# First chunk of x in two half loads, VectorE normalising the first three chunks, three constant products ahead on TensorE

## The reference

```python
xn = (x - mean(x)) / sqrt(var(x) + 1e-5)              # per row
# recurrent part, 256 inner columns
hidden, gate = split(xn @ W_hg)
h = scan over the 256 positions of each sequence:
        h[t] = sigmoid(-gate[t]) * h[t-1] + sigmoid(gate[t]) * (relu(hidden[t]) + 0.5)
s = h @ W_out
# mixture of experts, 16 experts of width 64, the two best per row, and a shared one of width 128
shared = (silu(xn @ Sg) * (xn @ Su)) @ Sd
p = softmax(xn @ Wr);  the two largest p and their experts
routed = sum over these two: p * (silu(xn @ Wg[e]) * (xn @ Wu[e])) @ Wd[e]
out = x + s * silu(routed + shared)
```

## Time and profile before

| | |
|---|---|
| median of 3 runs | 329.79 us (329.2 to 330.83) |
| profiled execution | 327.45 us |
| its span on the core | 325.7 us |
| PE busy | 291.7 us, 90% of the span |
| DVE busy | 252.0 us, 77% |
| ACT busy | 241.4 us, 74% |
| POOL busy | 201.2 us, 62% |
| chain that ended last | PE 78%, ACT 5%, issue 5%, POOL 4%, DVE 3%, DMA 1% |

### The profile page before, as it was taken

How to read it: one execution, slowest core, us unless ns; L and a number is a source line. 1 busy time by engine, 2 the same in 40 slices (tenths; PEclk the granted TensorE clock), 3 DMA queues, 4 the chain that set the end, 5 groups by cost and what they waited for, 6 DMA issues and landing times.

```text
span 325.7 us, 5997 instructions
## 1 busy us (share of the span) xinstructions
PE 291.7 (90%) x1523; PEld 198.5 (61%) x1523; DVE 252.0 (77%) x634; ACT 241.4 (74%) x517; POOL 201.2 (62%) x242
## 2 busy tenths in 40 slices
PE   0699999999989999996968999999999999999920
PEld 0357767766656666663645676777777777777620
DVE  7399999999999799999451778787878787878830
ACT  1789999999975777985664777777787878787520
POOL 3997446530137776878667777665656566656670
PEclk9999999999998999998999999999999999999985
DMA  8999999690006885333795435755656454541000
GB/s 233 303 372 393 440 445 399 228 432 3 0 28 204 279 256 215 124 127 147 247 405 195 168 107 194 208 176 149 180 149 181 150 181 129 168 127 51 19 0 0
DMA packets 28256, 63.62 MB, mean 195 GB/s; under 512 B 3717, under 2 KB 22672, under 8 KB 27456
## 3 DMA queue, kind: packets, MB, share of 16 engines
q1 hardware_dynamic: 21184, 45.58, 41.3%
q0 software_dynamic: 6752, 17.06, 14.2%
q10 hardware_dynamic: 288, 0.60, 0.6%
HBM read 29.32 MB, written 35.14 MB: 198 GB/s over the span
## 4 chain that ended last, share of the span: by engine, by line
PE 78%; ACT 5%; issue 5%; POOL 4%; DVE 3%; DMA 1%; POOLq 0%; ACTq 0%; DVEq 0%
PE p_u L998 21%; PE p_u L926 20%; PE p_s L1023 10%; PE p_s L937 8%; PE p_sh L1010 5%; PE p_lg L907 4%; PE p_sh L946 4%; PE p_xt L974 3%; POOL out L354 2%; PE p_xt L894 2%; DMA arena<-in_x 1%; POOL arena L310 1%; ACT arena L457 1%; ACT rec L427 1%; ACT rec L420 1%
## 5 line engine op out<-in xcount | busy, mean ns | idle before, releaser
L354 POOL DMA_INDIRECT out<-arena x83 | 82.1, 989 | 46.4 <-DVE arena L825 30.0
L926 PE MATMUL p_u<-xT,w_front 128*128 128x512 f32 x192 | 93.9, 622 | 3.2 <-DVE prod L569 2.5
L348 POOL DMA_INDIRECT slots<-arena,pos x64 | 71.4, 1116 | 28.7 <-issue 16.1
L998 PE MATMUL p_u<-arena 128*128 x166 | 78.3, 593 | 0.0
L926 PEld LDWEIGHTS p_u<-xT,w_front 128*128 128x128 f32 x192 | 34.9, 198 | 35.4 <-issue 33.9
L1023 PEld LDWEIGHTS p_s<-arena,rec 128*128 128x128 f32 x332 | 43.4, 191 | 21.2 <-issue 21.2
L799 DVE TENSOR_TENSOR rec<-p_u,rec 128x512 f32<-128x512 f32 (+1 forms) x42 | 28.8, 685 | 29.3 <-ACT rec L473 29.3
L480 ACT ACTIVATE rec<-p_sh 128x512 f32<-128x512 f32 (+1 forms) x42 | 24.9, 592 | 30.8 <-PE p_sh L1010 30.8
L1023 PE MATMUL p_s<-arena,rec 128*128 x332 | 44.1, 276 | 1.3 <-ACT rec L480 1.3
L998 PEld LDWEIGHTS p_u<-arena 128*128 128x128 f32 x166 | 28.3, 190 | 19.6 <-issue 19.6
L561 DVE TENSOR_TENSOR_SCAN rec<-rec 128x512 f32<-128x512 f32 x32 | 39.3, 1229 | 1.1
(11 more groups left out here) (130 smaller groups left out, 440.5 us busy)
## 6 DMA issues: line engine op xcount, KB each, us to landing
slots<-arena SPq DMA_DIRECT2D x4, 4116.0 KB, 27.0
arena<-slots SPq DMA_DIRECT2D x41, 392.0 KB, 3.3
arena<-in_W_lines SPq DMA_DIRECT2D x2, 2304.0 KB, 11.3
arena<-in_x SPq DMA_DIRECT2D x16, 256.0 KB, 5.3
arena<-in_W_lines SPq DMA_DIRECT2D x4, 768.0 KB, 4.5
out<-arena POOLq DMA_INDIRECT x83, 2.7
slots<-arena,pos POOLq DMA_INDIRECT x64
w_front<-in_W_front ACTq DMA_DIRECT2D x1, 392.0 KB, 3.6
```

The lines of the kernel that those rows point to most:

```text
L348: pool.indirect_dma_start(slots, index, xrow[:, t], None).then_inc(s_disp[t % WINDOW], 16)
L354: pool.indirect_dma_start(out, index, xg[:, n % RX, h, X], None, bounds_check=T - 1, oob_is_err=False)\
L926: nc.tensor.matmul(p_u[:, n % 4], w_front[:, UPS[q]:UPS[q] + P], xT[:, c % XB], start=True, stop=True)\
L998: last = nc.tensor.matmul(p_u[:, n % 2 * 2 + h], xsT[:, n % 2, h * P:(h + 1) * P], w_lines[:, bass.DynSlice(line_at[2 * n + h], 4 * P)], s ...
```

## The change

1. **Chunk 0** is loaded in two halves, one by SyncE and one by ScalarE, which issues it ahead of `w_front`. The wait of `ln_stats(0)` is for both.
2. **The first three chunks** (`HEAD`) are normalised by VectorE (`normalise_first`), with NBIAS made there too. GpSimd makes only RSTD for them (`rstd_first`, two instructions for four). ScalarE normalises from chunk 3 on.
3. **TensorE** first runs three products of 128x512 of a constant (`rec_v[:, 0]`, set to 1.0 by VectorE's first instruction, `s_warm`) into `p_u`, which later work overwrites.
4. **`STATS`** is later: chunk 4 between the two scans of iteration 0, chunks 2i+3 and 2i+4 in iteration i from 1 to 4, then 13 in iteration 5, 14 in 6 and 15 in 7.
5. **GpSimd** does the small constants and a part of the blank region (4 row groups) before the first `rstd`, and VectorE zeroes 6 groups in place of 10. GpSimd's larger zeroing of 11 groups now stands behind the `rstd_of` of chunk 3 and ahead of that of chunk 4.

```diff
-        BLANK_BY_DVE = SLOTS // 8
+        BLANK_BY_DVE = 6
+        BLANK_EARLY = 4
-        STATS = {i: [2 * i + 5, 2 * i + 6] for i in range(-1, 5)} | {5: [15]}
+        STATS = {i: [2 * i + 3, 2 * i + 4] for i in range(1, 5)} | {5: [13], 6: [14], 7: [15]}
...
-            for c in range(NCH):
+            sp.dma_start(xrow[:, 0:TT // 2, X], x_tiles[0][:, 0:TT // 2]).then_inc(s_xin[0], 16)
+            for c in range(1, NCH):
                 load_x(c)
...
+            def rstd_first(c):
+                pool.wait_ge(s_mv, c + 1)
+                if c >= 1:
+                    pool.wait_ge(s_rstd, c)
+                nc.gpsimd.tensor_tensor(var_eps[:, :], meanvar[:, c, :, 1], eps[:, :], ALU.add).then_inc(s_ve, 1)
+                pool.wait_ge(s_ve, c + 1)
+                nc.gpsimd.tensor_tensor(xrow[:, c * TT:(c + 1) * TT, RSTD], var_eps[:, :], minus_half[:, :], ALU.pow)\
+                  .then_inc(s_rstd, 1)
...
-            pool.wait_ge(s_const, 3)
-            rstd_of(0)
...
-            rstd_of(1)
+            nc.gpsimd.memset(rec_a.rearrange("p j (q n) -> p (j q) n", q=2)[:, :, 0:1], 0.0).then_inc(s_const, 1)
+            nc.gpsimd.memset(blank[:, BLANK_BY_DVE:BLANK_BY_DVE + BLANK_EARLY, 0:TOKEN], 0.0).then_inc(s_blank, 1)
+            pool.wait_ge(s_const, 3)
+            rstd_first(0)
...
-            rstd_of(2)
+            rstd_first(1)
+            rstd_first(2)
...
-            nc.gpsimd.memset(blank[:, BLANK_BY_DVE:, 0:TOKEN], 0.0).then_inc(s_blank, 1)
+            rstd_of(HEAD)
+            nc.gpsimd.memset(blank[:, BLANK_BY_DVE + BLANK_EARLY:, 0:TOKEN], 0.0).then_inc(s_blank, 1)
...
+            act.dma_start(xrow[:, TT // 2:TT, X], x_tiles[0][:, TT // 2:]).then_inc(s_xin[0], 16)
...
-            normalise(0)
             copy_xT(0)
-            for c in read(0):
-                normalise(c)
...
+            def normalise_first(c):
+                k, rows = c % 4, xrow[:, c * TT:(c + 1) * TT]
+                dve.wait_ge(s_rstd, c + 1)
+                nc.vector.scalar_tensor_tensor(out=rows[:, :, NBIAS], in0=meanvar[:, k, :, 0], scalar=-1.0,
+                                               in1=rows[:, :, RSTD], op0=ALU.mult, op1=ALU.mult).then_inc(s_nb, 1)
+                dve.wait_ge(s_nb, c + 1)
+                if c >= XN:
+                    dve.wait_ge(s_xt, c - XN + 1)
+                for t in range(TT):
+                    row = xrow[:, c * TT + t]
+                    last = nc.vector.tensor_scalar(xn[:, c % XN, t], row[:, X], row[:, RSTD:RSTD + 1],
+                                                   row[:, NBIAS:NBIAS + 1], ALU.mult, ALU.add)
+                last.then_inc(s_norm, 1)
...
+            nc.vector.memset(rec_v[:, 0], 1.0).then_inc(s_warm, 1)
             nc.vector.memset(blank[:, 0:BLANK_BY_DVE, 0:TOKEN], 0.0).then_inc(s_blank, 1)
-            for c in [0] + read(0) + STATS[-1]:
-                ln_stats(c)
+            ln_stats(0)
+            normalise_first(0)
+            ln_stats(1)
+            ln_stats(2)
+            normalise_first(1)
+            ln_stats(3)
+            normalise_first(2)
...
                 rec_scan(i, 0)
+                if i == 0:
+                    ln_stats(HEAD + 1)
...
+            pe.wait_ge(s_warm, 1)
+            for n in range(3):
+                nc.tensor.matmul(p_u[:, n], rec_v[:, 0, 0:P], rec_v[:, 0], start=True, stop=True)
             pe.wait_ge(s_const, 5)
             transpose_x(0)
```

More of the change, by code:

```diff
@@ L20 @@
 FIRST = 10
+HEAD = 3
 XN = 2
@@ L203, in recurrent_moe_block @@
         s_blank, s_init = sem("blank_rows_ready"), sem("slots_blanked")
+        s_warm = sem("warm_operand_ready")
         s_xin = [sem(f"x_landed{k}") for k in range(NCH)]
@@ L266, in load_slots @@
                 sp.dma_start(xg[:, n % RX, 0:m], rows.rearrange("(h p) w -> p h w", p=P)).then_inc(s_xg[n % RX], 16)
-            for c in range(NCH):
+            sp.dma_start(xrow[:, 0:TT // 2, X], x_tiles[0][:, 0:TT // 2]).then_inc(s_xin[0], 16)
+            for c in range(1, NCH):
                 load_x(c)
-            sp.wait_ge(s_blank, 3)
+            sp.wait_ge(s_blank, 4)
             for q in range(4):
@@ L303, in rstd_of @@
                 pool.wait_ge(s_mv, c + 1)
-                if c >= 1:
-                    pool.wait_ge(s_rstd, c)
-                    pool.wait_ge(s_nb, c)
+                pool.wait_ge(s_rstd, c)
+                pool.wait_ge(s_nb, c)
                 nc.gpsimd.tensor_tensor(var_eps[:, :], meanvar[:, k, :, 1], eps[:, :], ALU.add).then_inc(s_ve, 1)
                 nc.gpsimd.tensor_tensor(minus_mean[:, :], meanvar[:, k, :, 0], minus_one[:, :], ALU.mult).then_inc(s_ve, 1)
-                pool.wait_ge(s_ve, 2 * (c + 1))
+                pool.wait_ge(s_ve, HEAD + 2 * (c - HEAD + 1))
                 nc.gpsimd.tensor_tensor(xrow[:, c * TT:(c + 1) * TT, RSTD], var_eps[:, :], minus_half[:, :], ALU.pow)\
@@ L334, in _ @@
             nc.gpsimd.memset(carry[:, :, 0:1], 0.0).then_inc(s_const, 1)
-            nc.gpsimd.memset(rec_a.rearrange("p j (q n) -> p (j q) n", q=2)[:, :, 0:1], 0.0).then_inc(s_const, 1)
-            rstd_of(2)
+            rstd_first(1)
+            rstd_first(2)
             nc.gpsimd.iota(xrow[:, :, TOKEN:TOKEN + 2].bitcast(U32), [[P, NT], [0, 2]], base=0, channel_multiplier=1)\
               .then_inc(s_const, 1)
-            nc.gpsimd.memset(blank[:, BLANK_BY_DVE:, 0:TOKEN], 0.0).then_inc(s_blank, 1)
+            rstd_of(HEAD)
+            nc.gpsimd.memset(blank[:, BLANK_BY_DVE + BLANK_EARLY:, 0:TOKEN], 0.0).then_inc(s_blank, 1)
             nc.gpsimd.iota(blank[:, :, TOKEN:].bitcast(U32), [[0, SLOTS // 4], [0, ROW - TOKEN]], base=T, channel_multiplier=0)\
@@ L365, in block_weights @@
                 nc.gpsimd.tensor_tensor(xrow[:, a:b, W4:W4 + BLOCK], eq4[:, 0, 0:n], eq4[:, 1, 0:n], ALU.add).then_inc(s_w4, 1)
-            for c in range(3, NCH):
+            for c in range(HEAD + 1, NCH):
                 rstd_of(c)
@@ L533, in ln_stats @@
                 k = c % 4
-                dve.wait_ge(s_xin[c], 16)
+                dve.wait_ge(s_xin[c], 16 if c else 32)
                 for t in range(TT):
```

## The result

The changed kernel took 330.8 us in the median of 20 runs (326.09 to 332.35), the kernel before 329.31 in 20 runs beside it (324.52 to 331.17). The ratio is 1.0069, with a 95% interval of 1.0036 to 1.0102: slower by 0.7%, some 2.3 us. Forecast was 329.2, 0.2% faster. The time lies inside the range of 326.6 to 331.6, but the change went the other way; a slower kernel by more than the noise was given a chance of 0.15. The profiled execution took 329.53 us (span 327.8) against 327.45. (A ratio leaves disturbed runs out and is not that of the medians, and the profiles of the first experiment and of the kernels with six products and early statistics, with five products, and without products the second time are of disturbed executions, from which no time behind the prefix product is taken.

What follows compares the result with a forecast made beforehand. The chain was taken to run through TensorE from 21.07 us, with VectorE the bound at its prefix wait. Front -3.0, middle +2.07 and clock +0.3 made -0.6 us on the 329.79 median: 329.2 us, range 326.6 to 331.6.

Steps and rivals of the forecast that it cites:

- the front, the -3.0: Opening: logits of chunks 3 and 4 start at 28.4 instead of 31.67 us; gain taken as 3.0, between 2.3 and 4.0.
- rival 2: Opening: the products do not bring full clock to the transposes, or it falls before 8.3; 329.9 to 330.7 us; chance 0.20.
- the sum of -0.63: Whole kernel: front -3.0, middle +2.07 and clock +0.3, given in the prediction as -0.6 us.
- VectorE's normalising, 1.0: Opening: VectorE's NBIAS and four normalising instructions for chunk 0 were to take 1.0 us.
- The half loads: Opening: both halves of chunk 0 land in time for statistics at 4.2 us; by the skill's section, 5.0.
- The middle, +2.07: Iterations 6 and 7: one more set of statistics each, 1.25 us, with 0.43 hidden, delays the prefix product by 2.07.
- The clock after the wait, +0.3: Behind TensorE's wait at the prefix product: a longer wait costs 0.3 us more at low clock, between -0.7 and 1.5.
- the end I had at -0.7: Lower bound of the clock term behind the prefix wait: part of the slow stretch falls into the wait, -0.7 us.
- The slots, 0: Dispatch and slot loads: GpSimd falls 3.3 us behind TensorE, inside 3.8 us of reserve, so it costs nothing.
- The sign that I named: Near 200 us: no wait of ScalarE for slot rows; the forecast is wrong if ScalarE waits for pair 10.
- rival 1: Iterations 6 and 7: the two sets of statistics find cover, so the front's gain stays; 326.8 or 325.8 us; chance 0.15.
- faster by more: Whole kernel: a gain beyond the 1.65 us that a measurement can tell from no change; chance 0.27.

Runs made afterwards that it cites:

- the first experiment: The changed kernel with VectorE taking the statistics early again (chunk 15 in iteration 5, none in 6 and 7); ratio to the kernel before 0.997.
- five products: The changed kernel with five constant products, early statistics, and GpSimd's zeroing of carry and oh behind its third standard deviation; ratio to the kernel before 0.9916.
- chunk 15 behind dispatches: The changed kernel with GpSimd working out chunk 15's standard deviation behind the block weights and first four dispatches; ratio to the kernel before 1.0128.
- combined, no products: The changed kernel with early statistics, zeroing of carry and oh behind the third standard deviation, and no constant products; ratio to the kernel before 0.9965.

## Why the prediction was wrong

**The step that failed is the front, the -3.0.** "If TensorE is at full clock, they and the two products gain 0.5 + 1.7 more" rested on the clause that the engine "has been busy for 5 us when the transposes come". It had been busy from 1.5 to 6.0 and idle since. I had six passes at 0.9 us each from 2.25 to 7.5, because I gave them the low level throughout; they began 0.75 earlier and shortened when the clock rose, and the transposes came 0.59 later, so a gap of 0.8 us became one of 2.86. The 0.59 does not decide it: with the zeroing moved the gap was 2.09, and the clock fell as well. With the gap closed by three more products, the same step gives 2.94, and my 28.4 for the logits of chunks 3 and 4 is 28.73; with five products and the zeroing moved, my 16.9 for the paired logits is 16.77. So the walk through the engines was sound, and the clock's condition was not. This was my rival 2 (0.20): it names the fall "before 8.3", which is about where it came. Its 2.3 for the front was still too much: 0.87 in one execution and -1.0 in the other.

In the profiled execution the sum of -0.63 came out at +2.08, 2.7 us off: 2.13 by the front, -0.40 by the middle, and 0.98 by what lies behind the prefix, where I had 0.3 for the clock and 1.28 was measured. That the time still fell into the range is owed to its width.

**VectorE's normalising, 1.0**, measured 2.00, 1.11 without GpSimd's zeroing beside it. The Trainium skill, SBUF — State Buffer, section "Who interferes with whom", had this as a possible 0.8, with an exclusive lock of the ports that VectorE and GpSimd share; 0.89 was measured, and moving the zeroing removed it. That the lock is the reason was not tried. I left it out of the sum, though the two instructions of GpSimd stood in the code right behind the `rstd_first(0)` that releases VectorE.

**The half loads** brought more than expected: statistics from 3.80, against my 4.2. By the section "Issuing engines are not separate DMA queues" of the Trainium skill, DMA: Bandwidth & Descriptors, I had worked out 5.0. The row is against this 5.0, which took for granted that a half lands when the whole did: the halves were there by 3.5. It does not speak against the section. Whether the second issuer or the smaller piece did it was not tried.

**The middle, +2.07**, measured 1.67 in the changed kernel, 1.57 in the late statistics alone, both times, and 1.67 with six products (each from the logits of chunks 3 and 4 to the prefix). The mechanism was right and the size 0.4 too large. A set costs VectorE 1.19 with hand-overs, and 0.28 comes back: 1.19 + 1.19 - 0.43 - 0.28 = 1.67. The 0.28 is a small scan that took 0.48 beside GpSimd's routing weights before and 0.20 once these were later. The wait grew to 2.53, not 3.0.

**The clock after the wait, +0.3**: between prefix and the next group it cost less than before (3.55 for six passes against 4.13), because part of the low stretch fell into the wait. That was the end I had at -0.7. What I did not have is the clock in the second stage, where the 2.7 us stand.

**The slots, 0**, was right, and its steps nearly so. The first dispatch is 5.6 us later against the positions (I had 5.8) and 5.2 - 0.8 = 4.4 behind TensorE; by the third dispatch (102.08 against 97.90) 3.4 is left, for my 3.3. The load of pair 10 lands 0.79 after ScalarE wanted it, and TensorE's reserve covers that, as in the sum. The sign that I named, that ScalarE must not wait for pair 10, was a mistake: 3.3 us of lateness against the 2.3 in hand already said that it would.

The chances do not add up as told: rival 1 and a fifth of the forecast give at most 0.25 for "faster by more", not 0.27.

Together, at the points that TensorE passes, in us against the kernel before (paired logits at 21.07, prefix 97.04, the `ups` behind the wait for VectorE 152.30, first slot product 170.78, profiled time 327.45):

| | paired logits | prefix | 152 | slots | time | low clock, 90 to 310 us |
|---|---|---|---|---|---|---|
| changed kernel | -0.87 | +0.80 | +0.37 | -0.82 | +2.08 | 10.2 |
| the same again | +1.00 | +2.69 | +2.71 | +2.94 | +3.99 | 10.3 |
| chunk 15 behind dispatches | -0.96 | +0.99 | +2.63 | +2.83 | +3.06 | 10.2 |
| six products | -3.23 | -1.27 | -1.57 | -2.76 | -1.31 | 6.8 |
| combined, no products | -1.77 | -1.15 | -1.15 | -1.18 | -1.14 | 6.8 |

The last column is the time that the granted clock stood at 0.50 between 90 and 310 us, summed up from stretches of 1 us; the kernel before has 6.8. From the paired logits to the prefix the four executions with late statistics lose 1.67, 1.69, 1.95 and 1.96, the one with early statistics 0.62. Behind the prefix the two executions with as much low clock as before lose nothing (-0.04 and 0.01), and the three with 3.4 us more of it lose 1.28, 1.30 and 2.07. So the part of the loss that the wait at the prefix does not show goes with the length of the low stretches. What makes them longer is open: it is not the late statistics alone, since the kernel with six products has them too. So it is open as well why the late statistics alone cost 1.1% (3.9 us) in two groups when the middle shows 1.57: the late dispatch is excluded only in the changed kernel on other chips, and in those two groups the kernel before has no profile, while every other kernel has ScalarE's long idle times there. The late statistics alone were not run where these are missing.

## What to carry to other kernels

Work given to a cold TensorE paid here only when it lasted until the real work arrived: size it in passes at the level the clock reaches, not at the level it starts from. Before moving an instruction off a busy list, look for the wait that sets the end on that engine: 1.2 us of statistics had cover for 0.43 in iteration 6 and for none in iteration 7. And an engine that is 5 us late, and even makes another wait, may still cost nothing; the waits of the engine that sets the pace tell it, and taking the lateness away.

## What the hardware showed

- The granted clock fell to 0.50 at 8.3 us after TensorE had been busy from 1.5 to 6.0 and idle since; with products up to 9.4 it stayed at 1.00 through 15 us, and with products up to 7.8 and transposes at 8.13 as well.
- The column PEclk shows 1.00 from 0 us on although the first passes of a cold start take 1.0 to 1.2 us each against 0.47 later. Durations, not the column, tell the level at the start.
- GpSimd's zeroing of 820 bf16 columns, twice, stretched VectorE's four 128x128 float32 multiply-adds beside it from 1.11 to 2.00 us, although a zeroing reads nothing from SBUF.
- Three executions (the changed kernel twice, and chunk 15 behind the dispatches) with 3.4 us more of the low clock between 90 and 310 us than the kernel before lost 1.3 to 2.1 us there; two (six products, and the combined kernel) with no more of it lost nothing.
- Two executions of one kernel differed by 1.9 us at the paired logits (20.20 and 22.07), by the length of the low stretch alone, since the transposes before it started at 8.89 and 8.90.
